# A 3x3 convolution over eight images: every second band of rows by a minimal filtering form, the residual folded into the weights, PSUM seeded with the encoder's map

## The reference, cut to what matters

```
res  = conv3x3(gn(x), W_id, b_id)                 # 64 -> 64 channels, all 8 images
cA, cH, cV, cD = swt2_level3(gn(x)[0])            # wavelets of image 0 alone
dmt  = concat(attention(cA), attention(cH, cV, cD))
enc  = leaky_relu(conv3x3(dmt, W_enc, b_enc), 0.01)
out  = x + enc + res                              # enc is added to every image
```

## Time and profile before

| what | value |
|---|---|
| time, median of 3 runs | 1965.13 us (1960.27 to 1965.34) |
| span of the profiled execution, first to last instruction | 1957.5 us |
| PE busy | 1936.4 us, 99% of the span |
| DVE busy | 1465.0 us, 75% |
| ACT busy | 1008.3 us, 52% |
| POOL busy | 1032.8 us, 53% |
| moved by DMA | 391.94 MB, 200 GB/s over the span |
| encoder ends on PE, first matmul of band 0 | 792.05 us from the span's start |

### The profile page before, as it was taken

One profiled execution on the slowest core, in us unless ns is written; L12 is line 12 of the kernel. 1 busy time (PEld: TensorE's weight loads), 2 busy tenths in 40 slices (PEclk: granted clock), 3 DMA queues, 4 the chain that ended last, 5 costly groups with the idle time before them and its releaser, 6 DMA issues.

```text
span 1957.5 us, 79582 instructions
## 1 busy us (share of the span) xinstructions
PE 1936.4 (99%) x35562; PEld 1596.7 (82%) x35562; DVE 1465.0 (75%) x2253; ACT 1008.3 (52%) x1067; POOL 1032.8 (53%) x775
## 2 busy tenths in 40 slices
PE   9999999999999999999999999999999999999998
PEld 8987999999999999777877667767766667778896
DVE  5665578778778876677777777777777777777776
ACT  5546666666666666544444444434444444344442
POOL 0005988888888885444444444444444444444444
PEclk9999999999999999999999999999999999999999
DMA  9883698888888884688788787787887888887884
GB/s 172 256 291 82 185 271 221 213 220 205 216 217 218 200 220 95 150 199 208 203 198 198 203 207 199 202 202 200 199 207 200 203 199 207 201 203 198 209 208 124
DMA packets 132680, 391.94 MB, mean 200 GB/s; under 512 B 49708, under 2 KB 50480, under 8 KB 118160
## 3 DMA queue, kind: packets, MB, share of 16 engines
q1 hardware_dynamic: 132368, 387.10, 77.9%
HBM read 258.56 MB, written 128.45 MB: 198 GB/s over the span
## 4 chain that ended last, share of the span: by engine, by line
PE 36%; issue 33%; POOL 27%; ACT 1%; DMA 1%; POOLq 1%; DVE 1%; SPq 0%; DVEq 0%; ACTq 0%
POOL stage L1698 26%; PE ps L1106 14%; PE ps L1072 7%; PE ps L628 5%; PE ps L1076 5%; PE ps L1075 3%; PE ps L630 2%; POOLq L1696 1%; DMA pool_of<-in_x 0%; DMA big<-in_x 0%; POOL pool_of L1367 0%; POOL pool_of L315 0%; POOL pool_of L306 0%; PE ps L589 0%; ACT pool_of L1160 0%
## 5 line engine op out<-in xcount | busy, mean ns | idle before, releaser
L1698 POOL TENSOR_TENSOR stage<-stage,big 128x448 f32<-128x448 f32 x448 | 511.5, 1142 | 639.6 <-DVE stage L1673 639.6
L1610 PE MATMUL ps<-pool_of,w_hi 64*64 64x448 f16 x12096 | 640.5, 350 | 1.8 <-issue 1.5
L1610 PEld LDWEIGHTS ps<-pool_of,w_hi 64*64 64x64 f16 x12096 | 439.2, 107 | 152.1 <-issue 4.6
L1610 PE MATMUL ps<-pool_of,w_lo 64*64 64x448 f16 x8064 | 449.3, 350 | 1.6 <-issue 1.5
L1610 PEld LDWEIGHTS ps<-pool_of,w_lo 64*64 64x64 f16 x8064 | 297.4, 107 | 103.0 <-issue 5.3
L1673 DVE SCALAR_TENSOR_TENSOR stage<-ps,w_max,pool_of 64x448 f32<-64x448 f32 x448 | 305.8, 683 | 42.6 <-PE ps L1610 29.9
L1293 DVE BATCH_NORM_STATS2 pool_of<-big 128x6 f32<-128x448 f32 x392 | 232.5, 617 | 73.3 <-DMA big<-in_x 73.2
L1524 ACT ACTIVATE pool_of<-pool_of 128x2240 f16<-128x2240 f32 x56 | 126.6, 2262 | 309.8 <-PE ps L1610 309.8
L1673 DVE SCALAR_TENSOR_TENSOR stage<-ps,w_max,xs 64x448 f32<-64x448 f32 x384 | 262.2, 683 | 32.0 <-PE ps L1610 20.5
L1524 ACT ACTIVATE pool_of<-xs,pool_of 128x2240 f16<-128x2240 f32 x48 | 108.4, 2258 | 284.2 <-PE ps L1610 284.2
L1610 PE MATMUL ps<-big,w_hi 64*64 64x448 f16 x4032 | 224.0, 350 | 0.1
(11 more groups left out here) (199 smaller groups left out, 2494.8 us busy)
## 6 DMA issues: line engine op xcount, KB each, us to landing
out<-stage SPq DMA_DIRECT2D x448, 224.0 KB, 3.2
big<-in_x SPq DMA_DIRECT2D x392, 224.0 KB, 5.2
pool_of<-in_x SPq DMA_DIRECT2D x104, 560.0 KB, 6.7
xs<-in_x SPq DMA_DIRECT2D x96, 560.0 KB, 7.1
pool_of<-row_filtered SPq DMA_DIRECT2D x110, 224.0 KB, 3.7
row_filtered<-big SPq DMA_DIRECT2D x2, 6272.0 KB, 23.0
pool_of<-in_x SPq DMA_DIRECT2D x30, 392.0 KB, 8.1
row_filtered<-big SPq DMA_DIRECT2D x4, 1568.0 KB, 9.1
```

The lines of the kernel that those rows point to most:

```text
L1610: mm = pe.matmul(psum[4 * p + 2 * g + r][C * k:C * k + C, 0:NT], w[lanes, t, :], v[lanes, y:y + 2, kx:kx + W], start=(j == 0), stop=(j == ...
L1698: pool.tensor_tensor(stage[p][:, r, g, :], stage[p][:, r, g, :], e_map[:, e:e + NT], ALU.add)\
```

## The change

Of the 14 bands of an image, seven stay as they were ("direct": 0, 1, 3, 5, 7, 9, 11) and seven ("minimal": 2, 4, 6, 8, 10, 12, 13) are computed by F(2,3) along the rows: two output rows are made of four products over row combinations, not of six over rows. For rows d0 to d3 and the taps g0, g1, g2 the four products are m0 = (d0 - d2) g0, m1 = (d1 + d2)(g0 + g1 + g2)/2, m2 = (d2 - d1)(g0 - g1 + g2)/2 and m3 = (d1 - d3) g2; the even row is m0 + m1 + m2 and the odd row is m1 - m2 - m3. A minimal band is 4 products of 3 taps along the width x 3 f16 products x 4 quarters = 144 matmuls.

- DVE forms the sums (`neighbour_sums`, L1928 and L1929) and the differences (`differences`, L1935, in place in `xs`), ACT rounds them to f16 with the scale applied (`sums_high` L1871, `diffs_high` L1863), DVE writes the f16 rest (`sums_low` L1940, `diffs_low` L1946). The products m2 and m1 go into the banks `a_bank`. ACT copies -2 m2 away between them (`double`, L1879), DVE writes `b_bank = a_bank + that` (`seed_odd`, L1961), then m0 is added to `a_bank` and m3 to `b_bank`.
- PSUM is not cleared by a first matmul any more. ACT writes the encoder's map, scaled, into the banks ahead of the products (`seed_direct` L1633, `seed_minimal` L1893), and every matmul accumulates.
- The residual `x` is added by the convolution: the identity is added to the middle tap. Since the normalization differs for each image, six sets of three taps are made for each image and split into high and low f16 (`build_part`, L1734 to L1745, in two halves, at the two rounds of an image in which the third and the fourth direct band of that image are read out, for the next image).
- Read-out is one scaled copy: DVE for a direct band (`read_direct`, L1954, twice), ACT for the even rows (`even_rows`, L1886) and DVE for the odd rows (`odd_rows`, L1969, twice) of a minimal band. POOL does nothing in the loop but fill one halo row now and then. In the encoder POOL adds one map row to another for 14 of its 28 steps (`both_rows`).
- `xs` has three buffers, not six, and the loads are two or three bands ahead; `stage` has one buffer for direct and one for minimal bands. The loop's programs are written out on all engines.

The loop is now one of 56 rounds. Round q has direct band q+1 and minimal band q on PE, interleaved. The core of the diff:

```diff
-XS = 6
+XS = 3
+MINIMAL = (2, 4, 6, 8, 10, 12, 13)
+DIRECT = tuple(b for b in range(NB) if b not in MINIMAL)
...
             for step in range(NE):
...
+                if step > 1:
+                    both_rows(step - 2)
...
                 if step == NE - 1:
...
+                    ahead.spread(dve)
                     ahead.pads(dve)
-                    ahead.split(dve, 0, 0)
+                    ahead.build(dve)
+                    ahead.split(dve, 0)
...
                 if step == NE - 1:
                     pe.wait_ge(pads_set, 1)
+                    ahead.clear(pe, d[1][:, 0, 2, :, :].rearrange("p s w -> p (s w)"), range(4))
+                    ahead.spread_rows(pe)
...
-            ahead.conv(pe, 0, 0)
+            ahead.conv_first(pe)
             pe.wait_ge(ab_done, NE)
             pe.wait_ge(z_done, NE)
+            ahead.conv_rest(pe)
...
         def load(sp, k):
+            if k >= XS:
+                sp.wait_ge(split_done, k - XS + 1)
...
         def norms(dve):
...
+            step(dve.reciprocal(inv, norm_all[:, :, 0]))
+            step(dve.tensor_scalar(m_out, inv, w_max[:, 0:1], None, ALU.max))
...
+            dve.wait_ge(weights_in, 48)
+            for i in range(B):
+                ins = dve.tensor_scalar(diag[:, i, :], ident[0:C, :], r_out[0:C, i:i + 1], None, ALU.mult)
+            ins.then_inc(normed, 1)
...
+        def product(pe, i, s, v, rows_of, bank, last):
+            for kx in range(3):
+                for h, u in ((0, 0), (1, 0), (0, 1)):
                     for r in range(2):
                         lanes = slice(C * r, C * r + C)
                         for k in range(2):
+                            mm = pe.matmul(psum[bank + r][C * k:C * k + C, 0:NT], wt[i % 2][lanes, h, s, kx, :],
+                                           v[u][lanes, rows_of(k), kx:kx + W], start=False, stop=last and kx == 2 and u == 1, skip_group_check=True)
...
+        def product_m0(pe, j):
+            pe.wait_ge(b_seeded, j + 1)
+            pe.wait_ge(split_done, place_w(j) + 1)
...
         def sync(sp):
+            for q in range(NW):
+                store_direct(q)
+                if q:
+                    store_minimal(q - 1)
+                load(sp, 2 * q + 5)
+                load(sp, 2 * q + 6)
...
         def scalar(act):
+            for q in range(-1, NW):
+                if q >= 0:
+                    diffs_high(q)
+                if q >= 0 and q + 2 < ND:
+                    high(act, q + 2)
+                if q >= 0:
+                    double(q)
+                if q >= 0 and q + 2 < ND:
+                    full(act, q + 2)
+                if q + 2 < ND:
+                    seed_direct(act, q + 2, 0)
+                if q + 1 < NW:
+                    sums_high(q + 1)
+                if q >= 0:
+                    even_rows(q)
+                if q + 1 < NW:
+                    seed_minimal(q + 1)
+                if q + 2 < ND:
+                    seed_direct(act, q + 2, 1)
...
+            def read_direct(j, g):
+                i, b = direct(j)
+                if j:
+                    dve.wait_ge(stored[0], 64 * j)
+                dve.wait_ge(g_done, 2 * j + g + 1)
...
         def vector(dve):
...
+            for q in range(-1, NW):
+                if q > 0:
+                    odd_rows(q - 1)
+                if q >= 0:
+                    diffs_low(q)
+                if q + 1 < NW:
+                    neighbour_sums(q + 1)
+                i, b = direct(q + 1) if q + 1 < ND else (B, 0)
+                if i + 1 < B and b in DIRECT[2:4]:
+                    build_part(dve, i + 1, DIRECT.index(b) - 2)
+                if q + 1 < ND:
+                    read_direct(q + 1, 0)
+                if q >= 0 and q + 2 < ND:
+                    split(dve, q + 2)
+                if q >= 0:
+                    seed_odd(q)
+                if q + 1 < NW:
+                    differences(q + 1)
+                    sums_low(q + 1)
+                if q + 1 < ND:
+                    read_direct(q + 1, 1)
...
         def tensor(pe):
+            for q in range(NW):
+                j = q + 1
+                if j < ND:
+                    first_direct(pe, j)
+                product_m2(pe, q)
+                if j < ND:
+                    middle_direct(pe, j)
+                product_m1(pe, q)
+                if j < ND:
+                    last_direct(pe, j)
+                product_m0(pe, q)
+                product_m3(pe, q)
```

More of the change, by code:

```diff
@@ L77 @@
 Link = namedtuple("Link", "cleared einv_ready b32_in act_rows dve_rows first_split emx emax_part emax_all spread_max sx stat_in unit")
-Ahead = namedtuple("Ahead", "load dummies pads norms norm_first high full split edges root partners conv")
+Ahead = namedtuple("Ahead", "load weights_load dummies pads norms spread build normed high full split edges root partners sets spread_rows clear first_seed conv_first conv_rest")
 def input_transform():
@@ L1268, in scalar @@
                 if step == NE - 1:
[L1269 removed]
+                    ahead.high(act, 1)
                     scale(step)
[L1271 removed]
+                    ahead.full(act, 1)
                 if step:
@@ L1346, in vector @@
                     now += 1
-            ahead.split(dve, 0, 1)
+            ahead.split(dve, 1)
             outer(NE - 1)
@@ L1606, in conv, with build, clear @@
+        def build(dve):
+            for h in range(2):
+                build_part(dve, 0, h)
+        def clear(pe, data, banks):
+            for k in banks:
+                mm = pe.matmul(psum[k][:, 0:NT], data[:, 0:P], data[:, 0:NT], start=True, stop=True)
+            mm.then_inc(banks_set, 1)
+        def product(pe, i, s, v, rows_of, bank, last):
+            for kx in range(3):
+                for h, u in ((0, 0), (1, 0), (0, 1)):
                     for r in range(2):
@@ L1630, in store @@
                         row0 = HALF * s + R * b + 4 * k
-                        dst = out[bass.ds(i, 1), :, row0:row0 + 4, :]
-                        sp.dma_start(dst.rearrange("a c h w -> (a c) (h w)"), stage[p][C * k:C * k + C, s, :, :].rearrange("c g n -> c (g n)"))\
-                          .then_inc(stored[p], 16)
-            AHEAD = 4
-            with sp.Fori(0, B - 1) as i:
-                for b in range(NB):
-                    store(i, b)
-                    load(sp, i, b + AHEAD) if b + AHEAD < NB else load(sp, i + 1, b + AHEAD - NB)
@@ L1640, in sync, with store_direct, store_minimal @@
-            for b in range(NB):
-                store(B - 1, b)
-                if b + AHEAD < NB:
-                    load(sp, B - 1, b + AHEAD)
+                        sp.dma_start(out[i, :, row0:row0 + 4, :].rearrange("c h w -> c (h w)"),
+                                     stage[p][C * k:C * k + C, s, :, :].rearrange("c g n -> c (g n)")).then_inc(stored[p], 16)
+            def store_direct(j):
+                sp.wait_ge(g_read, 2 * j + 2)
+                store(*direct(j), 0)
+            def store_minimal(j):
+                sp.wait_ge(even_read, j + 1)
+                sp.wait_ge(odd_read, 2 * j + 2)
+                store(*minimal(j), 1)
@@ L1701, in main, with diffs_high @@
-        ahead = Ahead(load=lambda sp, b: load(sp, 0, b), dummies=dummies, pads=pads, norms=norms, norm_first=first_norm,
-                      high=high, full=full, split=split, edges=edges, root=root_of, partners=partners, conv=conv)
+            def diffs_high(j):
+                i, b = minimal(j)
+                act.wait_ge(diffs_ready, j + 1)
+                if j:
+                    act.wait_ge(odd_done, j)
+                act.activation(v_hi[:, 0:R, 1:1 + W], xs[place_w(j) % XS][:, 0:R * W].rearrange("p (r w) -> p r w", w=W), ACT.Identity,
+                               scale=norm_all[:, i, 0:1]).then_inc(diffs_hi, 1)
@@ L1703, in main @@
+        ahead = Ahead(load=load, weights_load=weights_load, dummies=dummies, pads=pads, norms=norms, spread=spread, build=build,
+                      normed=lambda act: act.wait_ge(normed, 1), high=high, full=full, split=split, edges=edges, root=root_of, partners=partners,
+                      sets=sets, spread_rows=spread_rows, clear=clear, first_seed=first_seed, conv_first=conv_first, conv_rest=conv_rest)
         return Programs(sync, tensor, scalar, vector, gpsimd), ahead
```

519 lines of the change are left out of this document (349 added, 170 removed).

## The result

| | median, us | range, runs | ratio to before |
|---|---|---|---|
| before | 1965.24 | 1960.27 to 1965.67, 4 | 1 |
| changed | 1816.66 | 1814.12 to 1823.04, 4 | 0.9254, interval 0.9233 to 0.9276 |
| forecast | 1834 | 1797 to 1900 | 0.933 |

The change takes 148.6 us off; 131 were forecast. The span of the profiled execution is 1813.1, where the sum had 1827.

The account below looks back on a forecast made before the run. PE's matmuls bound the old kernel; a DVE and ACT ring of 17.4 us a round would bound the new. Start 794.8, 54 rounds 939.6, weights 36.4 and smaller terms made a span of 1827, median 1834, range 1797 to 1900.

Parts of the forecast that it names:

- The two reads for which no row existed: Round's DVE read-out from PSUM, priced 1.17 us, and ACT's seed written into PSUM, priced 1.13, both without a matching profile row.
- The tail: End of the last round, which no direct band covers: products, odd rows, store issues and landing one after another, 17.9 us.
- The start: Seam from encoder to image loop: first matmul at 794.8, 2.7 us later than before, behind added DVE steps and weights.
- 8 us of stands: Loop start: PE stands 3 us before the second direct band, 1 before, and about 4 in round 0.
- the bound passes from PE to the ring: Image loop: the ring takes 17.4 us a round, 0.3 more than PE's ten runs of 36 matmuls (17.07).
- the ring: Dependent DVE and ACT steps from one round's `seed_odd` to the next, none able to start early, priced 17.4 us.
- hidden by nothing, as the ring has no slack: Making the next image's weights on DVE in the loop: 14 halves of 2.6 us add 36 us in full.
- The rival of a cheaper DVE: Loop: DVE costs less, perhaps by neighbours overlapping, so PE bounds rounds at 17.07 us; 1797 to 1816, chance 0.12.
- The clock: Loop rival: PE's clock halves after stands in weight rounds, 14 to 56 runs at 1.7 us more; 1858 to 1929, chance 0.05.
- The ten waits of PE: Ten waits on PE in a round where there were three, costed at nothing since 36-matmul runs showed no gap.
- the band of the ring as priced: Whole time if the ring holds at its priced length: 1816 to 1850 us, chance 0.60.
- The transfers: Loop rival: if 225 GB/s is all, rounds take 18.35 us, 1848; near 205, 20.1 us, 1940; chance 0.15.

Follow-up runs that it names:

- the run of the seam: Against the kernel with the rounding ahead of the last seed: second half of image 0's weights made behind band 0's `split`; 1794.87 us, 0.9148.
- the run of the ring alone: Changed kernel without the weights of images 1 to 7, 48 matmuls of each round and half of every store's bytes; 1755.55 us, 0.8945.

## Why the prediction was right, and which steps failed

**What held.** 4032 matmuls less shortened the round as was said, since PE stayed the bound (17.09 us for 17.07). The two reads for which no row existed were priced right: the read-out took 1.145 us for 1.17, the seed 1.10 for 1.13. `read_direct` waited once, 0.5 us, for a store, which landed after 3.6. The tail, from the end of the last round with a direct band (`odd_rows` released at 1795.91) to the span's end, is 17.2 us for 17.9.

**The start** came out 2.7 late. These rows of the changed kernel stand around it:

```profile
787.78 2.62 POOL L1396 TENSOR_TENSOR big<-big 128x896 f32<-128x896 f32 x1 [3.24 <-ACT big L1184]
788.59 2.42 DVE L1734 TENSOR_TENSOR pool_of<-pool_of 128x576 f32<-128x576 f32 x1
...
796.00 9.94 PE L1766 MATMUL ps<-pool_of 64*64 64x448 f16 x144 [4.17 <-DVE pool_of L1625]
```

The second half of the weights began with an instruction of 2.42 us, priced 0.74, beside POOL's addition; the first matmul came at 796.0, not 794.8. Round 1 starts on PE at 832.8, where the forecast had the end of round 0 at 830.1. So 1.2 of the 2.7 are the first matmul, and the other 1.5 lie behind it, where 8 us of stands were forecast and 9.5 came: PE ran at a granted clock of 0.50 from 796 to 801, behind its stand of 4.17 us, and then stood 1.78 for ACT's seed (L1633, at 812.12) and 1.63 for `double`. In the run of the seam PE came earlier and faster to the same seed, and stood for it until 811.95; so the lower clock cost next to nothing here.

**The step that failed** is "so the bound passes from PE to the ring", and with it "hidden by nothing, as the ring has no slack". Prices laid end to end made 17.41; laid start to start the same instructions make 16.62. The rival of a cheaper DVE, given 0.12, was the true mechanism, by the reason that was given for it: of the 0.79 us between, 0.62 is the overlap of neighbours and only 0.17 the prices. The Trainium skill, "VectorE: DVE Perf Modes", sections "The DRAIN you can't avoid" and "Two Vector instructions with no wait between them", has both halves: a flush between operations, and the exception that a next one which is not held starts earlier; the 0.07 to 0.10 us by which rows here start early agree with the exception. Rounds without weights are PE's 17.07, 18 us less over 54 of them, and the weights cost 24 in waits, not 36.4, since the ring's slack against PE, 0.45 us in a round, absorbed the rest.

**The clock** was a rival at 0.05: "halved for one run after each stand", 14 to 56 times, 1.7 us each. The price was right and the count too high: it fell three times in the loop, 5 us. A clock under 1.00 in the loop was also one of the signs of being wrong, and it came.

**A term that was missing.** The ten waits of PE were costed at nothing, from runs that showed no gap, and in the loop no wait of PE but the one for `seed_odd` shows. What cost time were stands in which PE waits for no other engine, some 15 us, and those no sentence had.

The sum, again by its parts: 832.8 to the end of round 0; 54 rounds from there to 1795.9, 963.1 us, against 979.0 forecast (939.6, 36.4 and 3); 17.2 behind. The 963.1 are 921.8 of matmuls (54 x 17.07), about 24 behind `seed_odd`, and 17 left: 5 for the clock and 12 for the stands. (The stands and waits of the weight loads sum to some 2 us more than that, since each includes the 0.07 us that always lies between two loads.) Against 1827 that is +2.7, -15.9 and -0.7. The other 3.4 between 1834 and 1816.7 lie outside: the median is now 3.6 above the profiled span, not 7.6.

**What was luck.** Rounds, weights and top bands were put some 33 us too high (17.8, 12.4 and 3), and the stands and the clock, which the sum left out, gave 17 back; without them the forecast would have missed by twice as much. The time lies 0.7 above the low end of 1816 to 1850, the band of the ring as priced, so that the number alone would speak for a mechanism that the traces rule out.

**The transfers** did not cap the loop: 231 to 239 GB/s went through, where 225 was feared. Their price came by another way, in PE's stands.

## What to carry to other kernels

Add up a chain start to start, not end to end: a tenth of a microsecond on each of eight links was the difference between a ring that bounds the loop and one that hides behind PE. When two candidates for the bound lie within 5%, lengthen one and lighten the other; work placed in the one that loses costs only what outruns its slack. Before work goes to an idle POOL, look whether DVE works on SBUF at the same moments; an order on ACT that shortens the wait gained more here. A wait of PE can cost more than its length when the clock falls behind it, as it did behind three of 13 here.

## What the runs showed of the hardware

**Stands of PE that shrink when data are left out.** The kernel before has them too (9.4 us of "issue" from 830 to 1800 at 202 GB/s). In the changed kernel two of them, as PE's weight loads show them:

```profile
1210.15 0.10 PEld L1766 LDWEIGHTS ps<-big,tail 64*64 64x64 f16 x1 [1.18 <-issue]
1223.38 0.14 PEld L1766 LDWEIGHTS ps<-big,tail 64*64 64x64 f16 x6 [1.23 <-issue]
```

From the end of the first to the start of the second are 1222.15 - 1210.15 = 12.0 us, and four other pairs lie as far apart within 0.1. At 47.4 ns a matmul that is about 253 matmuls, and with their weight loads 506 instructions. The page's instruction queue moved 140 packets of 16.4 KB from 900 to 1780 us, one each 6.3 us. That PE waits here for its own program, fetched by the DMA engines which the data keep 0.91 busy, fits both and the run without data; it is argued, since no run changed the fetch alone. The Trainium skill, "Runtime: NRT & Kernel Launch", section "Instruction fetch mechanics", says that an engine's program is refilled in blocks of 256 instructions through a DMA queue and that the cost is mostly hidden; here two blocks fit the spacing, and if the stands are this fetch, some 16 us of it were not hidden.

Nor do the bytes alone set the size: in the run of the ring alone, at 184 GB/s from 830 to 1780, the stands are larger, and why is open:

```profile
PEld ps L1766 <- issue: 32.5, 34, 3.1
```

**The clock behind a stand.** Of six stands of 2.4 us in one loop three were followed by the lower level (0.50), at 1.7 us each, and three were not. In the runs without these waits (the weights left out, the rounding ahead of the seed) the clock did not fall between 830 and 1780 us.

**DVE beside POOL**: rows of DVE lasted 2.10 for 1.15, 3.10 for 2.08, and at the seam 2.42 for the 0.75 us of the loop. It goes the other way too: in the run with the weights on POOL, while DVE's L1938 and L1939 ran on, the second at its usual 1.08, a multiplication on POOL (L1741, 64 elements, at 963.78) took 2.08 against a median of 0.44.
